# One strided VectorE reduction in place of four additions, for 13 of 28 batches of an edge sort

## What is computed

```python
xn = layernorm(x)
low  = relu(segment_sum(w1[:, None] * (xn @ W_low)[dst],  src, N))     # spmm by source node
high = relu(segment_sum(w2[:, None] * (xn @ W_high)[dst], src, N))
mlp  = relu(xn @ W_mlp)
x = x + gated_sum(low, high, mlp) + mix(xn)     # mix: linear attention over all nodes, then a small MLP
x = x + ffn(layernorm(x))                       # ffn only on the (N/2 - 1) nodes with the largest router weight
```

## Time and profile before

| | us |
|---|---|
| median of 3 runs | 1971.31 (1970.63 to 1973.62) |
| profiled execution, its own time | 1968.29 |
| profiled execution, span | 1966.5 |
| busy: POOL / PE / DVE / ACT | 1376.8 / 1567.2 / 1239.8 / 915.6 |

### The profile page before, as it was taken

The page is one execution under the profiler, slowest core; times in us unless marked ns, Lnnn a source line. Parts: engine busy times, 40 slices in busy tenths (PEclk is TensorE's granted clock), DMA queues, the critical chain, the costliest instruction groups (busy, mean ns, idle before and its releaser), DMA issues.

```text
span 1966.5 us, 30490 instructions
## 1 busy us (share of the span) xinstructions
PE 1567.2 (80%) x9109; PEld 1327.7 (68%) x9109; DVE 1239.8 (63%) x3136; ACT 915.6 (47%) x2641; POOL 1376.8 (70%) x1351
## 2 busy tenths in 40 slices
PE   3788888599998561788889888888888888889871
PEld 3466666588877561577777777777777777777750
DVE  8899999879988730345544554455454545545546
ACT  1688888677877550133333343333333334333323
POOL 4337778777777776777777777777777777777700
PEclk9899999789999785799999999999999999999975
DMA  3222221111121003433333333333333333333303
GB/s 89 83 66 68 68 68 49 40 36 47 48 66 47 6 6 95 133 102 105 100 102 103 104 101 105 105 101 100 102 103 103 102 103 105 100 102 105 103 14 131
DMA packets 102212, 162.99 MB, mean 83 GB/s; under 512 B 32190, under 2 KB 72762, under 8 KB 102040
## 3 DMA queue, kind: packets, MB, share of 16 engines
q0 software_dynamic: 55232, 113.59, 20.6%
q1 hardware_dynamic: 46808, 47.29, 7.6%
HBM read 139.76 MB, written 21.04 MB: 82 GB/s over the span
## 4 chain that ended last, share of the span: by engine, by line
POOL 31%; issue 13%; DMA 9%; DVE 2%; PE 2%; SPq 2%; ACT 1%; DVEq 0%; POOLq 0%; ACTq 0%
POOL arena L665 31%; DMA arena<-xn_rows,arena 9%; PE bank L1525 2%; SPq L558 1%; ACT side L1516 1%; POOL sorted_records L648 1%; DVE arena L1246 0%; DVE arena L1248 0%; DVE arena L1119 0%; DVE arena L1113 0%; SPq L563 0%; SPq L561 0%; DVE base L1288 0%; DVE arena L1253 0%; DVE arena L1245 0%
## 5 line engine op out<-in xcount | busy, mean ns | idle before, releaser
L1525 PE MATMUL bank<-arena 128*128 128x128 f32 (+3 forms) x6320 | 1145.1, 338 | 146.8 <-DVE arena L1119 74.4
L1525 PEld LDWEIGHTS bank<-arena 128*128 128x128 f32 (+1 forms) x6320 | 982.5, 188 | 287.8 <-issue 143.2
L665 POOL DMA_INDIRECT arena<-xn_rows,arena x852 | 840.7, 987 | 267.1 <-issue 246.1
L648 POOL DMA_INDIRECT sorted_records<-arena x448 | 512.9, 1145 | 218.0 <-issue 138.0
L1119 DVE TENSOR_TENSOR arena<-arena 128x640 f32<-128x640 bf16 (+1 forms) x204 | 164.4, 806 | 29.1 <-DVE arena L1113 0.2
L1113 DVE SCALAR_TENSOR_TENSOR arena<-io,arena 128x320 bf16<-128x320 f32 (+1 forms) x204 | 97.6, 479 | 96.5 <-issue 44.4
L1164 DVE CUSTOM_DVE_ANT_0 arena<-arena 128x256 f32<-128x256 f32 x98 | 37.8, 423 | 166.2 <-ACT arena L1449 166.2
L1169 DVE SCALAR_TENSOR_TENSOR att_prod<-sg,att_neg 128x9 f32<-128x9 f32 x49 | 8.4, 171 | 212.0 <-ACT sg L1457 212.0
L1525 PE MATMUL bank<-arena,base 128*128 128x128 f32 (+3 forms) x766 | 118.0, 287 | 22.0 <-ACT base L1304 13.8
L1525 PEld LDWEIGHTS bank<-arena,base 128*128 128x128 f32 (+2 forms) x766 | 110.2, 212 | 23.2 <-ACT base L1304 14.4
L1487 ACT ACTIVATE arena<-bank 128x256 f32<-128x256 f32 x49 | 18.8, 383 | 228.6 <-PE bank L1525 228.6
(11 more groups left out here) (311 smaller groups left out, 1918.2 us busy)
## 6 DMA issues: line engine op xcount, KB each, us to landing
arena<-xn_rows,arena POOLq DMA_INDIRECT x852
sorted_records<-arena POOLq DMA_INDIRECT x448
arena<-in_x SPq DMA_DIRECT2D x12, 512.0 KB, 4.1
xn_rows<-arena SPq DMA_DIRECT2D x12, 512.0 KB
x_plus_xn_rows<-arena SPq DMA_DIRECT2D x12, 512.0 KB
arena<-x_plus_xn_rows SPq DMA_DIRECT2D x12, 512.0 KB, 3.9
arena<-xn_rows SPq DMA_DIRECT2D x12, 512.0 KB
out<-base SPq DMA_DIRECT2D x4, 1024.0 KB
```

The lines of the kernel that those rows point to most:

```text
L648: pool.indirect_dma_start(rec_dram, bass.IndirectOffsetOnAxis(ap=idx[0:PR, par, u:u + 1], axis=0), stage_rec[0:PR, par, u * 8:(u + 1) * 8] ...
L665: pool.indirect_dma_start(gring[:, c % GR, :], None, xn_dram, bass.IndirectOffsetOnAxis(ap=rring[:, c, 3:4].bitcast(I32), axis=0)).then_in ...
L1525: return pe.matmul(out_, lhsT, rhs, start=start, stop=stop, **kw)
```

## The change

For batches g > MIX (g = 15 to 27, 13 of 28) the four additions are replaced by one `tensor_reduce` that reads `oh` as group, bucket, slot of the group, and sums over the innermost ten. Neighbours in that order lie 98 elements of two bytes apart. It raises `many_set` by 4 at once, so nothing that waits for it changes. Batches 0 to 14 are summed as before.

```diff
                 dve.wait_ge(S("oh_set"), g + 1)
                 wait(dve, S("rank_ready"), g)
-                h = oh[:, :, :].rearrange("p (s j) b -> p s j b", s=GROUPS)
-                H = GS // 2
                 with nc.allow_low_precision(reason="whole numbers up to ten"):
+                    if g > MIX:
+                        dve.tensor_reduce(many[:, :, 0], oh[:, :, :].rearrange("p (s j) b -> p s b j", s=GROUPS), AX.X, ALU.add).then_inc(S("many_set"), 4)
+                        return
+                    h = oh[:, :, :].rearrange("p (s j) b -> p s j b", s=GROUPS)
+                    H = GS // 2
                     dve.tensor_tensor(many[:, :, :, :], h[:, :, 0:H], h[:, :, H:GS], ALU.add).then_inc(S("many_set"), 1)
```

## The result

The changed kernel takes 1986.61 us (median of 4; 1985.76 to 1987.97) where the one before took 1972.39 us beside it (median of 4): ratio 1.0073, 95% interval 1.0056 to 1.0091. It is slower, by about 14 us; the forecast was 1982 us, 10.8 us more than before.

The account below looks back on a forecast made before the run. The prediction took GpSimd's scatters to set the pace from 444.17 us, with their end passing one for one to the kernel's end. The largest lateness term, 10.8 us, on the median 1971.3 gave 1982.1 us; range 1969.5 to 1989.

Parts of the forecast that it names:

- One for one to the end of the kernel: Second stage, entered from the last scatter: any delay of the scatters' end reaches the kernel's end in full, 10.8 us.
- The price of the reduction: The new reduction over 2940 elements on VectorE: 5.79 us at L707's 1.92 ns an element, between 3.21 and 6.27 us.
- d: Growth of a VectorE mixing slot, reduction less the four additions: 5.79 - 2.11 = 3.68 us, lower end 1.10, upper 4.16.
- term for batch 24: GpSimd's start of batch 24: late by -29.8 + 11d, 10.7 us with d = 3.68.
- The terms: GpSimd's starts of batches 14 to 24: lateness of VectorE's numbers less its lead; the largest, 10.8 us, delays the scatters' end.
- the loop through TensorE's ranks: In VectorE's mixing slot, ranks reach L766 through ScalarE: said not to change, with its constant 0.22 us wait.
- the relief of L748: Scatters held 0.20 us by L748 in each of 13 mixing slots would be freed: 2.7 us in all, left out.
- a loss of 1 us after batch 24: Last scatters: more of VectorE's work beside them after batch 24 may cost 1 us; left out.
- A free stride: Rival on the new reduction: no price for the stride, 3.2 us, d = 1.10, kernel 1969.7 us; chance 0.17.
- The smaller stride price: Rival on the new reduction: 5.1 to 5.5 us, d = 3.0 to 3.4, kernel 1977.4 us; chance 0.24.
- The additions' hold on GpSimd: Rival at the scatters: the additions' hold was the larger cost, removing it could give 1967 us; chance 0.05.
- The wait before L769: Sign in VectorE's slots: the wait for ScalarE, forecast before L766, shrinks from 4.65 us and its like to 0.2.

Follow-up runs that it names:

- the altered order with the reductions: The changed kernel's 13 reductions, with VectorE writing the mixing results after the destinations instead of before, against the kernel before: 2028.39 us, ratio 1.0290.
- the probes: Seventeen unread reductions over the one-hot tile at various steps, added to the kernel before after batch 0's sum: 1.04 ns an element in order, 1.80 at 24 bytes.
- the filler: The kernel before, additions kept in all 28 batches, plus an unread contiguous reduction of 2900 elements in the 13 batches of the change: 1988.23 us, ratio 1.0082.
- the repetition: The changed kernel run again with no edit, against the kernel before: 1989.32 us, ratio 1.0083.

## Why the prediction was right, and where it was off

**What bounds the kernel: shown.** The scatters are on the path; the delay at their end (10.65 us) appears at the first fetch unchanged (10.6). One for one to the end of the kernel holds only roughly: over the eight kernels and repetitions here the time moved by the delay of the last scatter, counted from batch 12, less 0.3 us (the reduction for batches 15 to 20) to plus 6.3 (the altered order with the reductions). Two readings of rows were a little off without bearing on the sum: 236.9 us for ten batches is 23.7 a batch and not 23, and VectorE's slots 16 to 20 hold 0.7 us of idle time each, of which the 0.22 us is the only wait.

**The price of the reduction: a term that was too large.** 5.79 us was forecast, 5.21 measured: 1.72 ns an element, not the 1.92 read off L707. The row was too short to carry a rate; at L707's step of 24 bytes the probes give about 1.8. The Trainium skill, Vector Engine (DVE) Microarchitecture Reference, section 5.2, has 1.73 ns a column for one source that hops 4 KiB at every element; the measured 1.72 agrees. Its 2.50 ns for steps of 24 words is for both sources or the output alone, which no run here has; one source at that step, 96 bytes, took 2.03 ns. With d = 3.10 for 3.68 the forecast's own term for batch 24 falls from 10.7 to 4.3 us: 6.4 us too much.

**The terms: right in form, with one path missing.** With the measured d = 3.10 they give 3.1, 4.5, 6.1, 5.0 and 4.3 us for batches 14, 15, 21, 23 and 24; counted from batch 12 the trace has 3.0, 4.4, 7.0, 6.7 and 6.7. The list left out batch 13, although the prediction has L826 late for it, and (g - 13) x d gives it nothing; it began 3.1 us late. The largest term does not change by that. The delay is set early, where VectorE's lead is thin, by the instruction's length and not by its kind (the filler). From batch 20 on the terms fall short by 0.8 to 2.4 us, because VectorE's slot did not stay at 23.5 us: the loop through TensorE's ranks, of which the prediction says that it does not change, took 0.8 us more in slots 20, 22 and 24, where TensorE ran at its lower clock. One such slot lies ahead of batches 20 and 21, two ahead of 22 and 23, three ahead of 24; with 0.8, 1.6 and 2.4 us added the terms give 6.9, 5.2, 6.6 and 6.7 us for batches 21 to 24, and the trace has 7.0, 5.2, 6.7 and 6.7. In the repetition the slower slots are 19, 21 and 23. There batches 19 to 21 fit in the same way (6.3, 6.9 and 7.7 against 6.3, 6.9 and 7.8), while batches 22 to 24 begin 2.5 us after L829 and not 0.85, because scatters were held. This path is read from the traces, which it fits to 0.1 us; no run tests it by itself.

**What was left out: a term put at nothing that was 4.2 us.** The prediction left out both the relief of L748 and a loss of 1 us after batch 24. L748 does hold nobody any more, nor does L799 (the old L796). But the scatters meet L811 at its beginning and not in its middle: from batch 13 on, the time beyond 0.956 us a scatter is 37.5 us before, 42.8 and 46.7 in the two traces of the changed kernel, 46.6 with the filler, which keeps the additions. A held scatter starts its successor at a time that the holding instruction sets, so the two engines fall into step. Up to batch 24, in the first trace, this costs nothing beyond VectorE's own lateness: counted from batch 12, the held time to the end of batch 23 is the same as before. After batch 24 has begun it adds 4.2 us (4.0 in the repetition), since VectorE, with no lead left, did its last two slots beside scatters that had run freer before: it is busy for 23.6 us beside batch 24 and 7.4 beside batch 25, instead of 15.3 and 1.0.

**The number at the last scatter: luck.** What the trace adds up to, counted from batch 12, is 4.3 (the term of batch 24 at d = 3.10) + 2.4 (TensorE's slower ranks) + 4.2 (held scatters at the end) = 10.9 us. The forecast was 10.8 because the price of the reduction was too high by 6.4 us there and 6.6 us were missing.

**The time: 4.6 us above the forecast, inside the range.** 1.1 us is the median of before, which came out higher beside the change. The rest, 14.2 less 10.65, or 15.7 less 12.3 in the repetition, is some 3.5 us that the scatters from batch 12 on do not explain. The second stage, which should have kept its length, is 1.4 to 5 us longer in the three traces with 13 reductions than in the others, the short one of before left out; yet the filler, with the same time as the changed kernel, has 1199.3. The first 390 us, which differ between traces, may have a part in it (in the repetition batch 12 begins 1.7 us later than before). Whether this is chance stays open.

**The rivals.** A free stride is refuted (1.72 against 1.04 ns). The smaller stride price was the true case for the instruction; its 1977.4 us lies 9 us under the measured time, for want of the terms above. The additions' hold on GpSimd was real, but taking them away gave nothing back: the filler keeps them and takes the same time.

**The signs.** VectorE's slots 16 to 19 took 23.5 us, 24.0 was forecast. Of the waits of 0.5 to 2 us forecast for batches 15 to 21 only that of batch 15 showed (1.65 us); from batch 16 on VectorE set the pace through held scatters instead. The wait before L769 shrank to 1.04 us where it did not reach 0.2. Scatters beside the reduction took 0.95 us, as forecast.

## What to carry to other kernels

Four additions that halve their data can beat one reduction that reads everything at one element a step; price a strided reduction from a row long enough to carry a rate, since an element at the steps of 16 to 196 bytes tried here cost 1.6 to 1.95 times as much as one in order. Where one engine feeds another through a small number of buffers, write the delay as the largest of (times delayed x extra length - lead) over the batches: the lead is thin at the start and covers later batches only. Then ask whether the longer slot leaves other engines idle for longer: here TensorE came back at half its clock in three slots, and each made VectorE wait 0.8 us more. And a lead is worth something twice: here GpSimd's scatters ran fastest while VectorE waited, so filling those waits for the last six reductions cost 3.5 us though nobody waited for the work.

## What the runs showed that I had not expected

- The step is free up to 8 bytes and jumps at 16: 1.04, 1.04, 1.04 and then 1.78 ns an element, for two-byte elements (nothing between 8 and 16 was tried); in four-byte words 1.04 at 8 bytes. 96 bytes is dearer (2.03) than 48 (1.72) or 192 (1.68).
- In slots 17 to 19 of the changed kernel GpSimd issues exactly 16 scatters to each 23.5 us of VectorE with only 0.30 us between two, so no wait shows, though the pace is VectorE's (each batch begins 0.85 us after L829): the waiting sits inside scatters that read 2.25 and 1.61 us instead of 0.96.
